# A megakernel's delta attention: the first levels of its triangular inverse in 32-token diagonal blocks

## The reference

```python
def step(S, inp):
    q_t, k_t, v_t, g_t, b_t = inp
    S = S * jnp.exp(g_t)[..., None]
    kv = jnp.einsum('bhk,bhkv->bhv', k_t, S)
    delta = (v_t - kv) * b_t[..., None]
    S = S + k_t[..., None] * delta[..., None, :]
    o_t = jnp.einsum('bhk,bhkv->bhv', q_t * scale, S)
    return (S, o_t)
```

## Time and profile before

| | us |
|---|---|
| median of 3 runs | 6400.4 (6397.15 to 6402.93) |
| the profiled execution, its time | 6396.97 |
| its span, first to last instruction | 6394.8 |

### The profile page before, as it was taken

One profiled execution on the slowest core, in us unless ns is written; L12 is line 12 of the kernel. 1 busy time (PEld: TensorE's weight loads), 2 busy tenths in 40 slices (PEclk: granted clock), 3 DMA queues, 4 the chain that ended last, 5 costly groups with the idle time before them and its releaser, 6 DMA issues. The chain is left out here.

```text
span 6394.8 us, 99261 instructions
## 1 busy us (share of the span) xinstructions
PE 5965.5 (93%) x37522; PEld 4271.9 (67%) x37522; DVE 3804.0 (59%) x7226; ACT 2694.1 (42%) x5584; POOL 2288.9 (36%) x2602
## 2 busy tenths in 40 slices
PE   5999999999999999997999999989999999999999
PEld 3777777777777777775677777643335667766665
DVE  6778787787877878773344444266634444444322
ACT  4554555545555455541355555215662122222221
POOL 4677777777777777772000000020000011111100
PEclk8999999999999999998999999989999999999999
DMA  0000000000000000000000000000001011121200
GB/s 30 5 5 5 5 5 1 5 5 5 5 5 5 5 5 5 1 1 15 15 11 13 14 11 9 20 7 1 1 1 53 18 64 64 64 70 64 71 7 7
DMA packets 33926, 112.56 MB, mean 18 GB/s; under 512 B 4273, under 2 KB 9649, under 8 KB 33457
## 3 DMA queue, kind: packets, MB, share of 16 engines
q1 hardware_dynamic: 33456, 106.22, 4.9%
HBM read 104.11 MB, written 2.10 MB: 17 GB/s over the span
## 5 line engine op out<-in xcount | busy, mean ns | idle before, releaser
L616 POOL TENSOR_TENSOR d_kq<-d_kq,d_tot 128x512 f32<-128x512 f32 x448 | 543.0, 1212 | 742.2 <-PE d_lpd L299 731.3
L683 DVE SCALAR_TENSOR_TENSOR d_qkv<-d_raw,d_wts,d_qkv 128x512 f32<-128x512 f32 x576 | 531.9, 924 | 43.1 <-ACT d_qkv L492 35.6
L299 PE MATMUL d_lpd<-d_kq,d_kF 128*128 128x128 f32 x3584 | 520.5, 290 | 33.9 <-POOL d_kq L646 27.2
L299 PEld LDWEIGHTS d_lpd<-d_kq,d_kF 128*128 128x128 f32 x3584 | 458.9, 199 | 58.0 <-POOL d_kq L646 26.7
L389 PEld LDWEIGHTS d_xy<-d_Tm,d_MA 128*128 128x128 f32 x3072 | 388.6, 196 | 92.3 <-issue 90.8
L389 PE MATMUL d_xy<-d_Tm,d_MA 128*128 128x64 f32 x3072 | 406.1, 276 | 43.9 <-ACT d_TT L517 43.9
L694 DVE COPY_PREDICATED d_MA<-d_pairs,d_lpd 128x512 f32<-128x512 int32 x384 | 317.6, 827 | 134.2 <-PE d_lpd L299 123.4
L1001 POOL TENSOR_TENSOR f1rstd<-f1var,mhalf 128x4 f32<-128x4 f32 x4 | 4.0, 1009 | 1090.1 <-DVE f1var L1026 1090.1
L1787 DVE TENSOR_REDUCE r_nm<-r_ps 128x2 f32<-128x1024 f32 x256 | 307.8, 1222 | 142.4 <-PE r_ps L1606 142.3
L290 PE MATMUL d_fr<-xnT,d_wts 128*128 128x512 f32 x768 | 367.1, 601 | 5.3 <-DMA d_wts<-in_headw 5.3
L1885 PE MATMUL e_pj<-xnT,e_wts 128*128 128x512 f32 x768 | 348.1, 603 | 14.3 <-DMA e_wts<-in_w3all 12.3
(11 more groups left out here) (422 smaller groups left out, 13654.3 us busy)
## 6 DMA issues: line engine op xcount, KB each, us to landing
e_wts<-in_w3all SPq DMA_DIRECT2D x64, 897.0 KB, 4.6
d_wts<-in_headw SPq DMA_DIRECT2D x16, 583.5 KB, 3.7
c_wqo<-in_wqo SPq DMA_DIRECT2D x32, 256.0 KB, 2.6
f3ws<-in_f3w SPq DMA_DIRECT2D x17, 384.0 KB, 8.2
f2ws<-in_f2s SPq DMA_DIRECT2D x16, 256.0 KB, 6.4
f2qs<-in_f2q SPq DMA_DIRECT2D x16, 256.0 KB, 6.7
f1ws<-in_f1w SPq DMA_DIRECT2D x8, 384.0 KB, 6.5
f0ws<-in_f0w SPq DMA_DIRECT2D x6, 384.0 KB, 5.6
```

Source lines behind the costliest of these rows:

```text
L299: last = nc.tensor.matmul(out[:, :, k], kF[:, u % 2, ch_(k)], moving[:, :, k, :, 1], start=True, stop=True)
L616: nc.gpsimd.tensor_tensor(v, v, bc(bc(t_l[:, :, 0], 2, h), 1, 2), ALU.mult)
L683: step = nc.vector.scalar_tensor_tensor(qkv[:, u % 3, x], raw[:, u % 2, x, i:i + GRP], tap(u, x, i), qkv[:, u % 3, x], ALU.mult, ALU.add)
```

## The change

Levels 0 to 4 pair blocks inside a diagonal block of 32 tokens, so all that is not zero lies in four 32x32 blocks per chunk. The change stores these levels compactly (`MB`, 128 partitions x 128 columns for four chunks: block row r on partitions 32r) and works on them with 32-wide tiles of the array. It also computes both factors `Tm` and `TT` by products, so that the transposes and copies of the levels go. Level 5 takes 32x32 tiles off the diagonal, level 6 takes 64x64 tiles. The factors live compactly in `TB` through level 4, and ScalarE spreads them and the output matrix to full width at levels 5 and 4. The rest of the kernel is as before.

```diff
+BL = 5
+BW = 1 << BL
+NB = P // BW
...
                 def products(u, lv):
                     h = 1 << lv
+                    if lv < BL:
+                        out = lpd[:, 0:P].rearrange("p (x c m h) -> p x c m h", x=2, c=NC, h=h)
+                        moving = kq[:, u % 2].rearrange("p x (c r m two h) -> p x c r m two h", c=NC, r=NB, two=2, h=h)
+                        for k in range(NC):
+                            for r in range(NB):
+                                last = nc.tensor.matmul(out[band(r), :, k], kF[:, u % 2, blk(k, r)], moving[:, :, k, r, :, 1], start=True, stop=True,
+                                                        tile_position=(0, BW * r), skip_group_check=True)
...
-                def transposed(u):
-                    for k in range(NC):
-                        last = nc.tensor.transpose(xy[:, ch_(k)], Tm[:, ch_(k)], T.ident[:])
-                    last.then_inc(tr_mm, 1)
+                def in_blocks(at_col, left, right, blocks, shift_in, shift_out):
+                    for k in range(NC):
+                        for r in blocks:
+                            i, o = band(r + shift_in), band(r + shift_out)
+                            last = nc.tensor.matmul(xy[o, at_col + k * BW:at_col + (k + 1) * BW], left(i, k, r), right(i, k, r), start=True, stop=True,
+                                                    tile_position=(i.start, o.start), skip_group_check=True)
+                    return last
...
-                        for j in range(NC):
-                            last = nc.tensor.matmul(mh(xy[:, j * 64:(j + 1) * 64], h), MA[:, lv, ch_(j)], even(Tm[:, ch_(j)], h), start=True, stop=True)
+                        if lv < 5:
+                            last = in_blocks(0, low_b(lv), Tb(1), range(NB), 0, 0)
+                        elif lv == 5:
+                            last = in_blocks(0, next_b, Tb(1), (0, 2), 0, 1)
+                        else:
+                            for j in range(NC):
+                                last = nc.tensor.matmul(xy[64:, j * 64:(j + 1) * 64], MA[0:64, 1, j * P + 64:(j + 1) * P], Tm[0:64, j * 64:(j + 1) * 64],
+                                                        start=True, stop=True, tile_position=(0, 64), skip_group_check=True)
                         last.then_inc(x_mm, 1)
...
-                                last = nc.tensor.matmul(xy[:, 256 + j * 64:256 + (j + 1) * 64], TT[:, ul % 2, ch_(j)], Xs[:, j * 64:(j + 1) * 64], start=True, stop=True)
+                        if lv < 5:
+                            in_blocks(P, Xb, Tb(0), range(NB), 0, 0)
+                            last = in_blocks(2 * P, Tb(0), Xb, range(NB), 0, 0)
+                        elif lv == 5:
+                            in_blocks(P, Xb, Tb(0), (0, 2), 1, 0)
+                            last = in_blocks(2 * P, Tb(0), Xb, (0,), 1, 1)
...
-                    if level and 1 <= lv < 6:
-                        pe.wait_ge(tm_ready, 5 * ul + lv)
-                        transposed(ul)
...
-                    if level and lv >= 2:
-                        act.wait_ge(tr_mm, 6 * ul + lv)
-                        nc.scalar.activation(odd(TT[:, ul % 2], h), odd(xy[:], h), ACT.Copy).then_inc(tt_ready, 1)
+                    if level and lv == 5:
+                        act.wait_ge(tb_ready, 4 * ul + 4)
+                        for r in range(NB):
+                            nc.scalar.activation(TT[band(r), ul % 2].rearrange("p (c r i) -> p c r i", c=NC, r=NB)[:, :, r], c3(TB[band(r), 0]), ACT.Copy)
+                        for r in range(2):
+                            last = nc.scalar.activation(Tm[band(r)].rearrange("p (c r i) -> p c r i", c=NC, r=2)[:, :, r], c3(TB[band(r), 1]), ACT.Copy)
+                        last.then_inc(t_spread, 1)
+                    if level and lv == 4:
+                        act.wait_ge(masked, 7 * ul + 5)
+                        for r in range(NB):
+                            last = nc.scalar.activation(MA[band(r), 2 + ul % 2].rearrange("p (c r i) -> p c r i", c=NC, r=NB)[:, :, r], c3(MB[band(r), BL + ul % 2]), ACT.Copy)
+                        last.then_inc(out_spread, 1)
...
-                    nc.vector.copy_predicated(into, bc(mh(pairs[:, lv], h), 1, 2), lpd[:].rearrange("p (x m h) -> p x m h", x=2, h=h)).then_inc(masked, 1)
+                    if lv == BL:
+                        dve.wait_ge(out_spread, u + 1)
+                    nc.vector.copy_predicated(into, bc(mh(level_pairs(lv), h), 1, 2), lpd[:, 0:2 * n].rearrange("p (x m h) -> p x m h", x=2, h=h)).then_inc(masked, 1)
...
-                        nc.vector.tensor_tensor(even(Tm[:], h), even(Tm[:], h), mh(xy[:, 256:512], h), ALU.subtract).then_inc(tm_ready, 1)
+                        if lv < 5:
+                            nc.vector.tensor_tensor(TB[:], TB[:], xy[:, P:3 * P].rearrange("p (x i) -> p x i", x=2), ALU.subtract).then_inc(tb_ready, 1)
```

113 lines of the change are left out of this document (70 added, 43 removed).

## The result

The changed kernel takes 6375.2 us in the median of 7 runs (6368.6 to 6380.4), the kernel before 6398.1 (6393.1 to 6402.9): ratio 0.9964, 95% interval 0.9952 to 0.9975. It is faster by 23 us. The forecast was 6285 us, 113 us faster: the sign was right, the size a fifth. The profiled execution has a span of 6366.8 us (before 6394.8) and a mean granted clock of 0.926 (before 0.977).

A forecast was written before the change was run, and what follows sets the result against it. It took each turn as a half set by GpSimd and a half set by TensorE. A gain of 2.3 us less 0.5 for the clock, 1.8 x 63 = 113 us, gave 6285 us; range 6160 to 6450.

The forecast's parts named there:

- the 9 us of TensorE: Whole turn: TensorE loses 9.1 us net of work, but the turn shortens by only 2.3 us.
- a first half that is GpSimd's alone: First half of a turn, set by GpSimd: unchanged at 22.4 us; the forecast is wrong if it moves.
- 1: Second half: the other chain gives way, half near TensorE's 16.4 us plus waits, 3.8 us a turn, 6155 us; chance 0.08.
- 2: No gain, within 0.2%: sets of 16 small products take 0.5 us or more, and clock falls; chance 0.07.
- the price of a group: TensorE: 16 small products, 32 MATMULs on four tiles, take 0.25 us, with 0.5 as the other end.
- Rival 4: TensorE: small products slower than counted; at 0.067 us each, 767 MATMULs take 51 us, 6850 us; chance 0.08.
- Rival 5: TensorE: diagonal tiles writing one bank don't run side by side; 1 us per 32 MATMULs, 6480 us; chance 0.03.
- The switch of tiling: TensorE between whole-array and tile steps: 0.09 us each, 31 more a turn, 2.8 us.
- the way to z: Second half: statistics at 7.05 us instead of 8.70, gain 1.65; statistics to z unchanged at 3.46 us.
- the rest is VectorE's own work: End of second half, z to the sums releasing GpSimd: gains at most 0.7 us, from 9.2 to 8.55.
- the clock, 0.5 us a turn: TensorE's new first-half waits, the last right before the second half, lower its clock: 0.5 us a turn, ends 0 and 2.5.
- rival 3: Second half: TensorE at 1.2 GHz for over 5 us makes it slower; at 10 us, 6570 us; chance 0.13.

The follow-up runs named there:

- nohorner_before: The kernel before without two of VectorE's four polynomial steps (terms 5 and 4, 1.4 us a turn): 6393.2 us, ratio 0.9995.
- fill3_after: The changed kernel with unused TensorE products ahead of its two long waits (three each) and the waits for R of chunks 0 and 1 (one each): 6299.1 us, 0.9844.
- thin_before: The kernel before with TensorE's small-level products and transposes made for one chunk of four, on the full array: 6547.2 us, ratio 1.0236.

## Why the prediction was right in sign and wrong in size

**Right in the main: who bounds the kernel, and that it is not the 9 us of TensorE.** 23 us came of them. nohorner_before bears out a part of the claim: with 1.4 us less on VectorE the kernel before does not move. The other part, a first half that is GpSimd's alone, held less well. The prediction named it as a sign of being wrong if that half moved, and its mean moved, from 22.7 to 23.1 us, and to 22.2 with the clock kept up. The 6375 us lie inside the wide range of 6160 to 6450, but outside the 6210 to 6350 of the likeliest case, so the account below is of a miss. Of the rivals, 1 is out (the half is 20.9 us, not near 16.4), and so is 2 in its reason: groups take 0.27 us, not 0.5.

**Right: the price of a group.** 0.25 us was taken, 0.27 measured, against an upper end of 0.5. Rival 4 is out: the turn shown has 797 MATMULs (260 + 537), which at its 0.067 would take 53 us, and it lasts 43.0; here 32 of them take 0.27, 0.0084 each. Nor does the Trainium skill's figure in "TensorE: Matmul & The Clock Gate", Part 1, of about 62 ns without hardware decode bind here. Rival 5 is out as well: sixteen products on diagonal tiles write one bank in 0.27 us, against the wording of Gotcha 1 in the Trainium skill's "TensorEngine Tiling (Array Packing)". The switch of tiling, 0.09 by the earlier trace rows, is nearer 0.15: a group and what follows it start 0.41 to 0.46 us apart. That is 31 times 0.06, some 1.9 us a turn that I had not counted. TensorE's busy time in the second half so fell by 3.3 us (21.42 to 18.16) where 5.0 were forecast; I take it that this cost little, as GpSimd waits for VectorE at the end of that half.

**Nearly right: the way to z.** Statistics at 7.05 forecast, 7.53 measured (8.70 before). The last small addition ahead of the V step (L864) took 1.37 us instead of 0.42, beside GpSimd's `scale` 2; I take that for the difference, and no run tests it. Statistics to z: 3.46 measured, as forecast.

**Wrong: "the rest is VectorE's own work", z to the roots 8.55 us.** Measured 9.6, with 9.3 before. kF did come earlier, by the 0.5 that the step allowed up to 0.7. But I took VectorE's durations from a trace in which GpSimd was silent at that moment, while my own step 1.65 us earlier moved GpSimd's scaling at level 5 beside the polynomial. This row was there to be worked out: `scale` 5 at 1553.77, the polynomial until 1553.74, three hundredths apart. The Trainium skill says it in "GPSIMD Engine Reference", section 1, Specifications: GpSimd's way to SBUF is shared with VectorE, and they get in each other's way when a VectorE instruction has two inputs in SBUF or runs in a mode with two ports. The runs agree in part. The polynomial and convolution steps (both inputs in SBUF) are stretched, the former by 0.88 us; mask 5 and T's update, which read one input from PSUM, stay at 0.72 and 0.42 beside GpSimd's scaling. But L864, with one input, is stretched from 0.42 to 1.37, and no row says whether it runs in a mode with two ports. The mask of level 1 in the kernel before, which reads PSUM, took 1.30 us in each turn beside a product of GpSimd's, for a reason no run shows. And beside the square roots no polynomial step was stretched, though both its inputs are in SBUF. The page would have changed the sum, and I did not weigh it.

**Wrong: the clock, 0.5 us a turn.** The cause was named rightly (7 us of new waits in the first half), the size and the place were not. fill3_after takes 76 us off the changed kernel, 1.2 us a turn, where 0.5 was taken and 2.5 the far end. Where I looked was wrong too: I feared for the wait right before the second half. The falls begin 42 to 45 and 0 to 3 us into the turn, and 12 to 14, behind the waits for T and for the first products, and nearly all of the low time lies in the first half; the second has 0.3 us a turn, far from the 5 us at which rival 3 becomes slower. The first falls slow the V projection (3.59 us instead of 1.9) and, through ScalarE's copies, w, but GpSimd hardly waits for w in the changed kernel (0.18 us in the mean of a turn, 0.15 before): it takes it up at 10.3 us, before at 10.4. What it waits for is the products of level 1, behind the head's output at the low clock: 0.85 us a turn. So GpSimd's half is GpSimd's only as long as TensorE is in time for it.

**The sum again, with measured terms.** Forecast 2.3 - 0.5 = 1.8 us a turn. With the clock kept up (fill3_after against before: 97 us, 1.54 a turn) the edit itself brings about 1.5 instead of 2.3; I put the difference to the stretched steps (0.88 a turn in the polynomial and, ahead of the statistics, L864), which the runs show, though no run shows this price by itself. Of the 1.5 the clock takes 1.2. The remaining 0.3 to 0.4 a turn are the 23 us measured. So the two terms were missed by about 0.8 and 0.7 us a turn, both to the same side, and together they left a fifth.

## What to carry to other kernels

When TensorE's work is cut, list which waits of it grow and what runs at half speed behind them: here the clock took back three quarters of a real gain, and 142 us of useless products brought it back. When a step comes earlier, look at what then runs beside it on the other engine: durations read from a trace hold only for the neighbours of that trace, and VectorE and GpSimd are no independent neighbours. And remove a little work from each engine's queue, in both kernels, to see who bounds: leaving out two steps told more here than all the moves.

## What the runs showed of the hardware

- A polynomial step of 512 columns with both inputs in SBUF took 0.69 us alone and 1.57 across two GpSimd products of `scale`, and the second of these 1.07 instead of 0.63: both lose. Beside GpSimd's square roots of 3.97 us the same step kept 0.69, in both kernels and every turn. A step with one input was stretched too (0.42 to 1.37).
- Less work on TensorE made a kernel slower by 2.4% (thin_before), with the granted clock at 0.87 instead of 0.99 over the same stretch; unused products made the changed kernel faster by 1.2% (fill3_after), with the clock at 0.98 instead of 0.87.
- Thirty-two small MATMULs on four tiles go in 0.27 us, but twice as many of them bring waits of up to 2.6 us within their rows, 213 us in 2500, in which TensorE waits for no engine.
